# Probabilities copied into a single-pass ring by transfers and transposed from there

## The reference

```python
xn = _layernorm(x)
kv_c = xn @ W_kvd + b_kvd                      # 64 columns
keys_c, values = heads(kv_c @ W_ku + b_ku, 128), heads(kv_c @ W_vu + b_vu, 128)
keys_r = _apply_rope(heads(kv_c @ W_kr + b_kr, 64))
q_c = xn @ W_qd + b_qd                         # 192 columns
queries_c, queries_r = heads(q_c @ W_qu + b_qu, 128), _apply_rope(heads(q_c @ W_qr + b_qr, 64))
scores = einsum('bhqd,bhkd->bhqk', concat(queries), concat(keys)) / sqrt(192)
probs = softmax(where(causal, -1e9, scores))
ctx = einsum('bhqk,bhkd->bhqd', probs, values)
x = x + ctx @ W_o + b_o + (xn @ binarize(weight).T + bias)
```

## Time and profile before

| | us |
|---|---|
| median of 3 runs | 1443.93 (1441.74 to 1444.32) |
| the profiled execution | 1439.73 |
| its span | 1437.9 |
| TensorE busy | 1396.2 (97%) |
| ScalarE busy | 1200.2 (83%) |
| VectorE busy | 1154.9 (80%) |
| GpSimd busy | 990.6 (69%) |

### The profile page before, as it was taken

The page is one execution under the profiler, slowest core; times in us unless marked ns, Lnnn a source line. Parts: engine busy times, 40 slices in busy tenths (PEclk is TensorE's granted clock), DMA queues, the critical chain, the costliest instruction groups (busy, mean ns, idle before and its releaser), DMA issues.

```text
span 1437.9 us, 27602 instructions
## 1 busy us (share of the span) xinstructions
PE 1396.2 (97%) x9786; PEld 1267.2 (88%) x9786; DVE 1154.9 (80%) x2756; ACT 1200.2 (83%) x2555; POOL 990.6 (69%) x573
## 2 busy tenths in 40 slices
PE   6889999999999999999999999999999999999997
PEld 4679999997899999998898999999889999999987
DVE  5868888886788888887677889887677888888887
ACT  4468888996788988898688888999778988888886
POOL 6776777777567777768765777777765777667750
PEclk9999999999999999999999999999999999999999
DMA  9751212212333222221333222221233322221100
GB/s 266 218 132 49 73 50 63 63 49 63 75 101 84 77 63 64 63 51 29 77 95 94 66 68 63 63 63 49 63 74 89 88 56 64 63 63 49 41 20 31
DMA packets 46958, 106.83 MB, mean 74 GB/s; under 512 B 9333, under 2 KB 17830, under 8 KB 46822
## 3 DMA queue, kind: packets, MB, share of 16 engines
q1 hardware_dynamic: 43360, 94.01, 25.7%
q0 software_dynamic: 3296, 11.01, 2.6%
q10 hardware_dynamic: 166, 0.03, 0.0%
HBM read 48.92 MB, written 9.96 MB: 41 GB/s over the span
## 4 chain that ended last, share of the span: by engine, by line
PE 84%; ACT 6%; DVE 4%; POOL 3%; DMA 2%; issue 1%; SPq 1%; DVEq 0%; POOLq 0%; ACTq 0%
PE turn L1494 16%; PE ring L1439 11%; PE ring L1471 8%; PE u_ps L1512 8%; PE ring L1469 8%; PE ring L1470 8%; PE u_ps L1513 8%; PE o_ps L1532 4%; PE o_ps L1533 4%; PE ring L1452 2%; ACT probs L755 2%; PE ring L1384 1%; PE ring L1378 1%; POOL k_rope L347 1%; DVE probs L1028 1%; ACT probs_hi L764 1%
## 5 line engine op out<-in xcount | busy, mean ns | idle before, releaser
L1028 DVE TENSOR_SCALAR_CACHE_REDUCE probs<-ring,c_t 128x1024 f32<-128x1024 f32 (+7 forms) x512 | 413.4, 809 | 103.6 <-PE ring L1471 99.8
L1038 DVE TENSOR_TENSOR probs_lo<-turn,probs_hi 128x512 fp32r<-128x512 f32 (+1 forms) x640 | 400.8, 630 | 68.8 <-ACT probs_hi L764 63.8
L764 ACT ACTIVATE probs_hi<-turn 128x512 fp32r<-128x512 f32 (+1 forms) x640 | 350.3, 549 | 112.1 <-PE turn L1494 106.1
L755 ACT ACTIVATE probs<-probs,row_min 128x1024 f32<-128x1024 f32 (+7 forms) x512 | 394.3, 771 | 11.8 <-DVE probs L1028 9.2
L1494 PE MATMUL turn<-ident,probs 128*128 128x128 f32 x2304 | 385.7, 275 | 6.0 <-ACT probs L755 3.7
L1494 PEld LDWEIGHTS turn<-ident,probs 128*128 128x128 f32 x2304 | 285.7, 140 | 31.7 <-ACT probs L755 9.2
L1512 PE MATMUL u_ps<-probs_hi,kv_nat 128*128 128x256 f32 x1152 | 313.2, 301 | 0.0
L1513 PE MATMUL u_ps<-probs_lo,kv_nat 128*128 128x256 f32 x1152 | 288.8, 280 | 0.0
L1469 PE MATMUL ring<-k_hi,q_hi 128*128 128x512 f32 (+2 forms) x768 | 279.9, 364 | 0.0
L1471 PE MATMUL ring<-k_hi,q_lo 128*128 128x512 f32 (+2 forms) x768 | 263.6, 343 | 0.0
L1470 PE MATMUL ring<-k_lo,q_hi 128*128 128x512 f32 (+2 forms) x768 | 262.9, 342 | 0.0
(11 more groups left out here) (218 smaller groups left out, 2566.8 us busy)
## 6 DMA issues: line engine op xcount, KB each, us to landing
swapped<-k_rope SPq DMA_DIRECT2D x128, 128.0 KB, 2.3
wv<-wv_scratch SPq DMA_DIRECT2D x62, 256.0 KB, 4.1
wp<-wp_scratch SPq DMA_DIRECT2D x62, 192.0 KB, 3.5
wp<-wp_scratch SPq DMA_DIRECT2D x31, 256.0 KB, 3.1
swapped<-q_y SPq DMA_DIRECT2D x62, 128.0 KB, 2.3
swapped<-q_x SPq DMA_DIRECT2D x62, 128.0 KB, 2.3
k_hi<-qb_kv_hi SPq DMA_DIRECT2D x16, 256.0 KB, 3.7
k_lo<-qb_kv_lo SPq DMA_DIRECT2D x16, 256.0 KB, 4.6
```

Of the source, the lines that this page charges most:

```text
L755: act.activation(p, p, ACT.Exp, scale=-1.0, bias=row_min[:, r:r + 1], accum_out=row_sum[:, g % 4, w, h:h + 1]).then_inc(exp_ready, 1)
L764: act.activation(probs_hi[:, r % 4, 0:width], turn[r % 2][:, 0:width], ACT.Identity).then_inc(turned_hi, 1)
L1028: dve.tensor_scalar(probs_of(g, w, h), ring[slot_of(entry)][:, KEY_COLUMN[qt]:KEY_COLUMN[qt] + keys], c_t[b % 2][:, qt, ds(pair * 2 + h, 1 ...
L1038: dve.tensor_tensor(probs_lo[:, r % 4, 0:width], turn[r % 2][:, 0:width], probs_hi[:, r % 4, 0:width].bitcast(F32), ALU.subtract).then_inc ...
```

## The change

- `ident` becomes a view of `ident_words`, a tensor of the single-pass format with the same bits.
- `probs` has one set of two buffers in place of two sets. New are `words`, for each head a ring of 13 tiles of 128 columns in the single-pass format. SP copies each item's probabilities into it with one transfer, or two where the ring wraps (`load_words`), after the exponential, and where needed after the transposes that last read those tiles.
- `turn_group` waits for both heads' copies, reads `words` and `ident_words`, and writes `turn` as the single-pass format. The bits are passed on, and the parts are taken from them as before.
- `minimum` waits for the copies that read the buffer which it writes.
- `probs_hi` and `probs_lo` have 3 slots in place of 4 (`DEEP`).
- The orders of TensorE, ScalarE, VectorE and SP are written anew; transposes and what follows them stand up to a block later; swaps, weight loads and stores stand between the copies. `DRAIN` is 4. The stores of a batch's results come later.

```diff
-DRAIN = 3
+DRAIN = 4
+TILES = NT + 1
+WORDS = 13
+DEEP = 3
...
-        ident, ident_bf, mask_bf = sb("ident", [P, P]), sb("ident_bf", [P, P], BF16), sb("mask_bf", [P, P], BF16)
+        ident_words, ident_bf, mask_bf = sb("ident_words", [P, P], F32R), sb("ident_bf", [P, P], BF16), sb("mask_bf", [P, P], BF16)
+        ident = ident_words[:, :].bitcast(F32)
...
-        probs = [[sb(f"probs{i}{h}", [P, (NT + 1) * P]) for h in range(2)] for i in range(2)]
-        probs_hi, probs_lo = sb("probs_hi", [P, 4, 512], F32R), sb("probs_lo", [P, 4, 512], F32R)
+        probs = [sb(f"probs{h}", [P, TILES * P]) for h in range(2)]
+        words = [sb(f"words{h}", [P, WORDS * P], F32R) for h in range(2)]
+        probs_hi, probs_lo = sb("probs_hi", [P, DEEP, 512], F32R), sb("probs_lo", [P, DEEP, 512], F32R)
...
+            def load_words(g, *items):
+
+                for x in items:
+                    h, w = divmod(x, 2)
+                    first, tiles = words_of(g, w)
+                    sp.wait_ge(exp_ready, g * SCORE_ITEMS + x + 1)
+                    if first + tiles > WORDS:
+                        sp.wait_ge(turn_full, group_of_tile(first + tiles - 1 - WORDS) + 1)
+                    for to, start, some in words_pieces(g, w):
+                        sp.dma_start(words[h][:, to * P:(to + some) * P].bitcast(F32),
+                                     probs_of(g, w, h)[:, start * P:(start + some) * P]).then_inc(words_loaded[x], 16)
...
-                if m + 1 < STEPS:
+                if more:
                     if pair == PAIRS - 1:
                         stack(b + 1)
                     swap(m + 1, 0)
...
+                load_words(g, 0, 1, 2)
...
+                load_words(g, 3)
+                if more:
                     swap(m + 1, 1)
...
+                load_words(g + 1, 0)
                 if m + 2 < STEPS:
                     load_wp(m + 2)
...
+                load_words(g + 2, 0, 1)
+                if more:
                     load_wv(m + 1)
...
+                if g > 0:
+                    dve.wait_ge(words_loaded[x], WORDS_LOADED[w][g - 1])
+                    if w == 0 and qt > LONG_SHORT[(g - 1) % BLOCKS][0]:
+                        dve.wait_ge(words_loaded[x + 1], WORDS_LOADED[1][g - 1])
...
                 if first_kt == 0:
-                    pe.wait_ge(exp_ready, g * SCORE_ITEMS + 3 + w)
+                    for h in range(2):
+                        pe.wait_ge(words_loaded[h * 2 + w], WORDS_LOADED[w][g])
...
-                        mm = pe.transpose(turn[r % 2][:, (2 * t + h) * P:(2 * t + h + 1) * P],
-                                          probs_of(g, w, h)[:, kt * P:(kt + 1) * P], ident[:, :])
+                        at = (words_of(g, w)[0] + kt) % WORDS
+                        mm = pe.transpose(turn[r % 2][:, (2 * t + h) * P:(2 * t + h + 1) * P].bitcast(F32R),
+                                          words[h][:, at * P:(at + 1) * P], ident_words[:, :])
```

```diff
                 if n == 0:
                     project(g, ROPE_K)
-                    output(g - 3, 1)
-                    turn_group(g - 1, 0)
-                    turn_group(g - 1, 1, (g, 0))
-                    weigh_group(g - 2, 3)
-                    weigh_group(g - 2, 4)
+                    weigh_group(g - 2, 0)
+                    turn_group(g - 2, 3)
+                    weigh_group(g - 2, 1)
+                    turn_group(g - 2, 4, (g, 0))
+                    weigh_group(g - 2, 2)
                     head_ready(g, 0)
                     scores(g, 0, 0)
                     scores(g, 0, 1)
-                    turn_group(g - 1, 2, (g, 1))
-                    output(g - 2, 0)
-                    weigh_group(g - 1, 0)
-                    weigh_group(g - 1, 1)
+                    output(g - 3, 1)
+                    turn_group(g - 1, 0)
+                    weigh_group(g - 2, 3)
+                    turn_group(g - 1, 1, (g, 1))
                     scores(g, 1, 0)
```

316 lines of the change are left out of this document (172 added, 144 removed).

## The result

The kernel after takes 1757.85 us (median of 4 runs, 1755.63 to 1761.21) against 1443.93 before: 1.2183 times as long, 95% interval 1.2165 to 1.2200. Forecast were 1372.5 us and a range of 1334 to 1458. The profiled execution took 1759.88 us, 1758.1 of it span.

The account below looks back on a forecast made before the run. TensorE, busy 97%, was taken to bound the kernel, with ScalarE next. From 1439.7 us profiled, 76.4 came off and 5 were added, giving 1368.3; 4.2 more for the median made 1372.5 us, range 1334 to 1458.

Parts of the forecast that it names:

- The transposes: TensorE's 2304 single-pass transposes: each falls from 0.108 to 0.058 us, saving 115 us of TensorE, 3.6 us per pair.
- the start to start inside a group: Sign on TensorE: spacing of transposes within a group, 0.058 us if the forecast holds or 0.11 if not.
- The rival of the held transpose: TensorE: single-pass transposes held by a plain 4-byte load at 0.111 us; 7 us more plus 5, 1456 us; chance 0.14.
- ScalarE at 95% of a plain pair: ScalarE, 35.4 us of work, limits plain pairs to 37.3 us, a gain of some 2.6 us each.
- The copies' duration: Probability copies inside SBUF: 512 KB land about 4.9 us after issue, at 208 GB/s; 22.7 us per pair.
- the copies set the pace: Rival: copies land late behind swaps and weight loads, plain pairs stay at 39.3 us; 1430 us; chance 0.12.
- Wait (1): VectorE's minima wait for copies out of their buffer: free, 4.9 us copy against 5.8, 0.9 us to spare.
- the chain of copies stalls each block: Rival: copies over 5.8 us make minima late, 1.2 us per block, 154 us; about 1520 us; chance 0.09.
- Wait (2): Copies into the 13-tile ring wait for transposes, transposes for copies: 4.9 us fits a 9.3 us block; cost nothing.
- Wait (3): On SP, the q swap stands behind the copy of the block's fourth item: 1.6 us to spare for a later swap.
- Start and end: First copy ahead of any transpose and a drain of four blocks' orders: 5 us, between 2 and 10.
- A transposing load of 190 ns: Sign on TensorE: a transpose's load lasting 190 ns, in place of 140, would sink the forecast.

## Why the prediction was wrong, point by point

| step, in the order in which it was added | median, us | difference |
|---|---|---|
| before | 1442 | |
| single-pass transposes, old orders | 1425 | -17 |
| new orders, three slots of parts | 1577 | +152 |
| copies made, not waited for | 1608 | +31 |
| SP's waits for the ring | 1612 | +4, not clear of noise |
| transposes wait for the copies | 1740 | +128 |
| exact probabilities, one buffer set, the ring in SBUF: the kernel after | 1758 | +18 |

The differences hold for this order of adding; the ring's waits are worth 4 or 57 depending on it. The three rows with copies ahead of the last copy to DRAM, as said above.

**The transposes** (0.108 to 0.058 us, 115 us of TensorE): mis-sized. Measured is 0.092 in the same reckoning. The step that failed is the bound taken from one place, the transpose that starts 0.05 us after its load behind a mask: it showed how soon a matmul may start after *its* load, not how fast loads follow each other. The 140 ns against 190 of a plain load were read as 50 ns less of rate; in truth the spacing of these loads is 83 to 87 ns, some 25 less than the 111 of the earlier trace rows. The bounds 0.058 and 0.111 held it. The sign that was to show it, the start to start inside a group, would have misled: its median fell from 0.109 to 0.064 us, close to the forecast, because the first loads of a group are made ahead, and the time came back at the matmul behind the group. The rival of the held transpose had the right mechanism, a bound by the load, with the price of a plain load, 0.111, and so a loss of 7 us where there was a gain of 17.

**ScalarE at 95% of a plain pair** was never reached. With old orders it was 35.3 of 39.2 us, 90%, since the transposes gave too little. Whether 95% would have been possible stays open.

**The copies' duration** (4.9 us for 512 KB, from 208 GB/s and a 256 KB landing of 3.7): too slow for most copies, about right for those that count. In the plain pair 149 GB/s at a share of 0.48 are 310 GB/s at full, not 208. The page of the kernel after has the medians from issue to landing:

```profile
words<-probs SPq DMA_DIRECT2D x90, 256.0 KB, 2.3
words<-probs SPq DMA_DIRECT2D x42, 448.0 KB, 3.1
words<-probs SPq DMA_DIRECT2D x30, 512.0 KB, 3.0
```

The number of transfers, 650 for 128 blocks, is the five per block that were reckoned. So the typical copy is faster than assumed and the mean DMA share is moderate, and still waiting for the copies costs over 100 us. The mean hides that the copies that TensorE waited for took 4.4 us, at DMA shares of 0.80, 0.94 and 0.86 in the waits shown, and nearly all of them were issued right behind loads of weights or spread keys. The rival "the copies set the pace" named this ("words land late behind swaps and weight loads"), but priced it as a smaller gain, 1430 us. Whether the bursts make the ways long or only go with them was not tested.

**Wait (1)**, the minima behind the copies, called free with 0.9 us to spare: about right. VectorE waited 29.7 us in the whole span for copies (23 times), while it had hundreds to spare. The rival "the chain of copies stalls each block" rested on this wait and a copy of over 5.8 us; no such copy is typical, and its 1520 us would have come from VectorE's waits, while the loss came from TensorE's.

**Wait (2)**, the transposes and the ring, "the new orders move them nearly a block later, so that 4.9 us fit in a block of 9.3. Taken at nothing": this is the step that failed worst among the waits, 128 us, or 132 with the 4 of the ring. Setting a flight time against a block's length leaves out the exponential that ends late, SP's order, in which a copy waits behind swaps, loads and the copies ahead of it, and the ring. And the room was not a block. Medians from the traces, from the end of the third item's exponential, for the four blocks of a pair:

| us, from the end of the exponential | first | second | third | fourth |
|---|---|---|---|---|
| kernel before: first transpose of the long row starts | 0.5 | 0.4 | 0.1 | 0.5 |
| new orders, no copies: it starts | 7.4 | 6.3 | 3.7 | 4.4 |
| kernel after: TensorE is free for it | 7.3 | 6.5 | 3.9 | 4.4 |
| kernel after: the copy is issued | 0.0 | 2.3 | 1.4 | 0.3 |
| kernel after: the copy has landed | 3.2 | 7.2 | 6.1 | 3.0 |

The new orders gave 3.9 to 7.3 us of room, not 9.3, and the copies of the second and third block needed 7.2 and 6.1. Those are the two blocks in which TensorE waits. The 4.9 us for the way itself were not the error: the awaited copies took 4.4. SP's own waits show what it spends its time on:

```profile
SPq L471 <- PE turn L1557: 514.1, 174, 9.7
SPq L473 <- ACT probs L811: 254.8, 190, 7.6
SPq L406 <- ACT q_y L726: 146.1, 31, 6.1
```

514 us is the ring waiting for transposes: each head's ring has 13 places and a block takes 9, so each copy takes places that the block before used. Everything behind such a wait in SP's queue waits too. The size of this wait is not its price: SP also waited 409.0 us for the ring where that cost 4 us, and without the ring's waits it stood 795.0 us for exponentials instead of these.

**Wait (3)**, the q swap behind the fourth item's copy, 1.6 us to spare: taking the swaps out of SP's queue changed nothing (1757.97 us), so it held. Not foreseen was SP's lateness at a change of batch, where TensorE stands 7 us for the stacking transfers, 22 us in all.

**The orders** had no term. The prediction priced what the change adds and where a copy fits, but took the orders of four engines, rewritten by hand, as carrying what they carried before. That was the largest error, 152 us, half of the loss. With the runs in hand the diff can be read so: the new ScalarE order puts a high part, which waits for a transpose, between a finished projection and its evacuation, and TensorE's next mask wants that slot; u's high part stands behind two exponentials, and TensorE's weigh_group(g - 1, 0), which wants the place of that u, comes 0.8 us of work after the last matmul that writes it. Both are of one kind: who is queued behind a waiting instruction, and who waits for him. That it could have been read off the diff beforehand is argued here, not shown.

**The clock** had no term either. Before, TensorE did not stand still in the plain pair, and the earlier trace rows show 1.00 throughout. Behind a long stall it loses again: 97 us more busy time in the kernel after (1470.6) than in the run with the same transposes, the old orders and 44 us of idle time (1373.4), close to the 93 by the mean clock.

**Start and end** (5 us) were not measured apart.

**Arithmetic.** Two sums of the rivals are off and change nothing: a plain pair that stays at 39.3 us gains 0.5 us, not 0.6, so 16 us and 1434 in place of 1430; and gains of 1.6 to 3.3 us over 32 pairs give 1350 to 1405, not 1345.

Of what was to show each step: plain pairs at 37.3 us (48.3), ScalarE near 95% (76% of a plain pair), DMA share 75 to 85% (48%), TensorE's idle time put down to copies (115 of 287.5 us), minima waiting for copies (little), GpSimd's waits for swaps growing (yes: from 145.4 to 289.5 us for k_rope's; with the swaps on GpSimd they were 90.7, at the same time of the kernel, so they cost nothing here). A transposing load of 190 ns, which "would sink the forecast", didn't come.

The only version that beats both kernels is the one with the old orders, no copies and probabilities rounded before the transpose: 1424.64 us, 1.1% below before, at the price of the low parts.

## What to carry to other kernels

An order written by hand for several engines is a change by itself, however small the rest: for every entry that moves, ask what it waits for, what is queued behind it, and which slot that frees. Test it alone, with the data path of the kernel before, before a new data path is put on it. A copy put between two engines is not paid by its typical duration: what counts is when the reader wants it, how long the late ones take beside other transfers (4.4 us against 2.6 here), its place in an in-order queue and the depth of its buffer; a ring of 13 tiles for blocks of 9 ties each block to the one before. And a stall of TensorE costs more than it lasts when the clock falls behind it; in smaller pieces apart from each other (3.2 us in four pieces of a plain pair) it cost only itself.

## What the runs showed of the hardware that was not expected

- Transposing loads of the single-pass format last as long as those of the two-pass format (141 and 140 ns) and follow each other every 83 to 87 ns, against 111 ns of plain 4-byte loads. So halving the passes of a 128-column transpose brought 0.108 only to 0.092 us.
- Copies of 256 to 512 KB inside SBUF over 128 partitions land in 2.3 to 3.1 us after issue; 512 KB in 3.0 us are some 170 GB/s for a single transfer, latency included. The 58 copies that TensorE waited for took 4.4 us.
- The granted clock goes from 1.00 to 0.50 behind a stretch in which TensorE was busy 2.43 of 4.40 us (behind one with 0.54 of 3.30 in the kernel after), and stays there for some 3 us. In the run with four shorter waits, 0.4 to 1.5 us and apart from each other, it stayed at 1.00 over the plain pair. Removing two of those waits while the third grew from 1.5 to 2.0 us made the kernel no faster.
